# The spectrum's product in the tokens stage, second component made by ScalarE and GpSimd instead of VectorE

## The chip, the cores and the metric

The kernel runs on one core of one Trainium2 chip. The metric is the device time of one execution in microseconds (us). The engines are called PE (TensorE, the matmuls), DVE (VectorE), ACT (ScalarE), POOL (GpSimd) and SP (the queue that issues the DMAs).

## The reference, cut to what matters

The program is a convolution block over 32 images of 96 channels and 56x56 pixels, and then, on each image seen as 3136 tokens of 96 channels, a Fourier mixing layer and an MLP. Only the mixing layer matters here:

```python
h = relu(bn(layernorm(t) @ w1.T))              # 3136 tokens, 192 channels
X = jnp.fft.fft(h, axis=1, norm='ortho')
rd, idg = jnp.diagonal(r), jnp.diagonal(i)
xr = relu(X.real * rd - X.imag * idg + rb)
xi = relu(X.imag * rd + X.real * idg + ib)
y = ifft(xr + 1j * xi).real
o = bn(y @ w2.T)
```

h is real, so the spectrum is computed for half of the frequencies, and the other half follows from its conjugate: each product is needed with a plus and with a minus sign (a sum and a difference).

## The kernel before, in words

Up to 2700 us of the profiled execution the program sets up its constants and does the convolution. The rest is the tokens stage (`tokens_stage`, L1037). It is a software pipeline over the images: the work of one image is spread over five turns (`LAGS`), and in each turn every engine does a part of up to five images. The order on each engine is written out by hand: `PLACES` (L980) gives every step its places in a plan of 2000 slots a turn, and `tensor_turn`, `scalar_turn`, `pool_turn` and `vector_turn` walk through the slots and issue what stands there, modulo 2000. An engine works strictly in that order; semaphores hold it wherever an input is not ready. A turn is marked in this text by its first L1239 matmul.

The spectrum of an image comes in six groups (`XG`, L1111): groups 0, 2, 3 have 8 frequencies of 128 channels, group 5 has 5 of them, groups 1 and 4 ("wide") hold the 64 other channels of two frequencies in one slot, 8 and 7 slots. A slot is 56 numbers per partition, so groups have 448, 448, 448, 448, 392 and 280 numbers. For each group:

- PE (`spectrum_tensor`, L1299; matmuls L1311 for wide groups, L1314 for the others) writes real and imaginary parts to the PSUM tensor `bank_x`, of which there is one. It waits until the group before has been read out of it (`sd_done`, L1306).
- ACT (`scaled_scalar`, L1410) reads the real part and writes two scaled copies with bias to `d_minus` (L1415, L1417).
- DVE (`real_vector`, L1573) adds the scaled imaginary part, with plus to `s_plus` (L1580) and with minus in place in `d_minus` (L1582), for the first and then for the second component: four `scalar_tensor_tensor`, each with one PSUM and one SBUF input.
- ACT (`relu_scalar`, L1420; L1425) takes the ReLU of both halves of `s_plus`.
- DVE (`fold_vector`, L1585; L1593, twice a group) folds `d_minus` and `s_plus` into `zp` or `zq`: both inputs are in SBUF.

Other steps that the text speaks of:

- PE: `w1_tensor` L1359, `stage1_tensor` L1368, `w2_tensor` L1322/L1323, `stage3_tensor` L1329, `stage4_tensor` L1339, layer norm sums L1239, L1244, L1257, L1263, `mlp1_tensor` L1296, `mlp2_tensor` L1350, and `spread_tensor` L1269, which spreads a row of means (`mrow`, `spread_mean_tensor`, needs the MLP's copies `h16_done`) or of reciprocal deviations (`rrow`, `spread_rstd_tensor`, L1283, needs `xc_done`) over the channels.
- DVE: `centre_vector` (`xc`, L1629), `norm_vector` (`yq`, L1638), `bias1_vector` (L1605), `relu1_vector` (L1612), `residual_vector` (`tb`, L1648), `var_vector` (L1597, L1599), `rt` (L1624), copies `wz` L1672 and `cc` L1680.
- ACT: `h16_scalar` L1432, `bn3_scalar` L1507, `squares2_scalar` L1469, `h_scalar` L1501, `a_scalar` L1494, `std1_scalar` L1442.
- POOL has two steps only: `prep_pool` (L1551), after `bn3_scalar`, and `out_pool` (L1559), each a `tensor_tensor` with both inputs in SBUF.

Of the kernel before, what the change touches and what calls it, by code (L numbers as in the profile page):

```python
# [17 lines left out]
ALU = mybir.AluOpType  # L18
ACT = mybir.ActivationFunctionType
# [8 lines left out]
W = 56  # L28
# [11 lines left out]
TP = 2 * W  # L40
# [11 lines left out]
def wait_count(eng, sem, value):  # L52

    if isinstance(value, int) and value <= 0:
        return
    eng.wait_ge(sem, value)
# [44 lines left out]
def build(nc, x4, cw1, g1, b1, cw2, g2, b2, cw3, g3, b3, aw1, bn1g, bn1b, bn1m, bn1v, ar, ai, arb, aib,  # L101
# [13 lines left out]
    with keep:  # L115
# [857 lines left out]
        with st:  # L973
            tokens_stage(nc, st, NB, x, out, z3_d, t_d, a_d, c_d, t1_d, t4_d, g2_d, g3_d, mean_w, s3, w1a, w2p, w2q,
                         w2shift, diag, fq1, fq2, fqb1, fqb2, epsc)
# [22 lines left out]
 'spectrum': (3861, 3995, 4323, 4618, 4907, 5029),  # L998
 'act_scaled': (3910, 4039, 4372, 4679, 4947, 5091),
 'dve_real': (3935, 4127, 4412, 4705, 4969, 5312),  # L1000
 'act_relu': (4002, 4174, 4506, 4752, 5011, 5379),
 'dve_fold': (4027, 4238, 4646, 4926, 5125, 5398),
 'w2': (4475, 4707, 4851, 5070, 5391, 5570, 5667, 5811),
# [33 lines left out]
def tokens_stage(nc, st, NB, x, out, z3_d, t_d, a_d, c_d, t1_d, t4_d, g2_d, g3_d, mean_w, s3, w1a, w2p, w2q, w2shift,  # L1037
                 diag, fq1, fq2, fqb1, fqb2, epsc):

    def sb(name, shape, dt=F32):  # L1040
        return st.enter_context(nc.sbuf_tensor(name, shape, dt))

    def sem(name):
        return st.enter_context(nc.semaphore(name))
# [15 lines left out]
    bt = sb("bt", [TP, KH, H])  # L1060
    sp_t = sb("s_plus", [128, 2, 2, 8, W])
    dm_t = sb("d_minus", [128, 2, 2, 8, W])
    zp = sb("zp", [128, 2, 8, TP])
    zq = sb("zq", [128, 8, TP])
    wz = sb("wz", [TP, 2, 4 * C])
# [15 lines left out]
        for k, n in (("w1", 1), ("s1", 1), ("x", 2), ("c", 1), ("o", 1), ("l0", 1), ("l1", 1))]  # L1081
    LL = (L0, L1)
    xs = X[:, :, :].rearrange("p a (s c) -> p (a s) c", c=128)
# [10 lines left out]
    x_full, ace_done, s0_done, sd_done, s1p_done, d1_done, r_done, z_done = (  # L1094
        sem(k) for k in ("spectrum", "spectrum_scaled", "sum_real", "diff_real", "sum_imag", "diff_imag", "relu_plus",
                         "z_done"))
# [14 lines left out]
    XG = ((0, 0, 8), (1, 0, 8), (0, 8, 8), (0, 16, 8), (1, 8, 7), (0, 24, 5))  # L1111
# [3 lines left out]
    def here(s, name, live):  # L1115
        return [(at[name].index(s + NT * lag), lag) for lag in range(len(live))
                if live[lag] and s + NT * lag in at[name]]
# [181 lines left out]
    def spectrum_tensor(pe, m, g):  # L1299
        wide, k0, n = XG[g]  # L1300
        if wide:
            for k in ((0, 1), (2, 3))[k0 // 8]:
                pe.wait_ge(ld_b[k], m * 16 + 16)
        else:
            pe.wait_ge(ld_b[k0 // 8], m * 16 + 16)
        wait_count(pe, sd_done, m * 6 + g)  # L1306
        for s in range(n):
            if wide:
                for e in range(2):
                    k1 = min(2 * (k0 + s) + e, KH - 1)  # L1310
                    ins = nc.tensor.matmul(xs[64 * e:64 * e + 64, s, 0:TP], bt[:, k1, 128:192], g2c[:, :],  # L1311
                                           start=True, stop=True)
            else:
                ins = nc.tensor.matmul(xs[:, s, 0:TP], bt[:, k0 + s, 0:128], g2c[:, :], start=True, stop=True)  # L1314
        ins.then_inc(x_full, 1)
# [56 lines left out]
    def tensor_turn(pe, tau, par, live):  # L1372
        for s in range(NT):
            for p, lag in here(s, "spread_mean", live):
                spread_mean_tensor(pe, tau - lag, p)
            for p, lag in here(s, "spread_rstd", live):
                spread_rstd_tensor(pe, tau - lag, p)
            for k, lag in here(s, "mlp1", live):
                mlp1_tensor(pe, tau - lag, k)
            for g, lag in here(s, "spectrum", live):  # L1380
                spectrum_tensor(pe, tau - lag, g)
            for c, lag in here(s, "stage4", live):
                stage4_tensor(pe, tau - lag, c)
            for r, lag in here(s, "mean1", live):
                mean1_tensor(pe, tau - lag, (par + lag) % 2, r)
            for r, lag in here(s, "square1", live):
                square1_tensor(pe, tau - lag, r)
            for r, lag in here(s, "mean2", live):
                mean2_tensor(pe, tau - lag, r)
            for r, lag in here(s, "square2", live):  # L1390
                square2_tensor(pe, tau - lag, r)
            for c, lag in here(s, "mlp2", live):
                mlp2_tensor(pe, tau - lag, c)
            for u, lag in here(s, "w2", live):
                w2_tensor(pe, tau - lag, u)
            for u, lag in here(s, "stage3", live):
                stage3_tensor(pe, tau - lag, u)
            for g, lag in here(s, "stage1", live):
                stage1_tensor(pe, tau - lag, g)
            for g, lag in here(s, "w1", live):  # L1400
                w1_tensor(pe, tau - lag, (par + lag) % 2, g)
# [8 lines left out]
    def scaled_scalar(act, m, g):  # L1410
        wide, k0, n = XG[g]
        re = xs[:, 0:n, 0:W]
        act.wait_ge(x_full, m * 6 + g + 1)
        wait_count(act, z_done, (m * 6 + g - 1) * 2)
        nc.scalar.activation(dm_t[:, g % 2, 0, 0:n, :], re, ACT.Identity, bias=diag[:, wide, 2:3],  # L1415
                             scale=diag[:, wide, 0:1]).then_inc(ace_done, 1)
        nc.scalar.activation(dm_t[:, g % 2, 1, 0:n, :], re, ACT.Identity, bias=diag[:, wide, 3:4],  # L1417
                             scale=diag[:, wide, 1:2]).then_inc(ace_done, 1)

    def relu_scalar(act, m, g):  # L1420
        wide, k0, n = XG[g]
        act.wait_ge(s0_done, m * 6 + g + 1)
        act.wait_ge(s1p_done, m * 6 + g + 1)
        v = sp_t[:, g % 2, :, 0:n, :]
        nc.scalar.activation(v, v, ACT.Relu).then_inc(r_done, 1)  # L1425
# [118 lines left out]
    def prep_pool(pool, n, par, c):  # L1544
        pool.wait_ge(bn3_done, n * NCH + c + 1)
        if c == 0:
            wait_count(pool, w1_full, (n - 1) * NG)
            wait_count(pool, st_t, (n - 1) * 16)
        to = y[0:C, par, :, ROWS * c:ROWS * c + ROWS, :].rearrange("p j a b -> p a j b")
        v, xv = (q[:, c % 3, :].rearrange("p (a j b) -> p a j b", a=ROWS, b=2) for q in (zin, xin))  # L1550
        nc.gpsimd.tensor_tensor(to, v, xv, ALU.add).then_inc(y_done, 1)  # L1551

    def out_pool(pool, b, c):
        pool.wait_ge(ob_done, b * NCH + c + 1)
        if c == 0:
            wait_count(pool, st_out, b * 16)
        to = onat[:, :, 8 * c:8 * c + 8].rearrange("p a (j b) -> p j a b", b=2)
        v, o = (q.rearrange("p (j a b) -> p j a b", j=4, b=2) for q in (tb[:, c * CH:c * CH + CH], o16[:, c % 4, :]))
        nc.gpsimd.tensor_tensor(to, v, o, ALU.add).then_inc(out_done, 1)  # L1559

    def pool_turn(pool, tau, par, live):
        for s in range(NT):
            for c, lag in here(s, "pool_y", live):
                prep_pool(pool, tau - lag, (par + lag) % 2, c)
            for c, lag in here(s, "pool_out", live):
                out_pool(pool, tau - lag, c)

    @block.gpsimd
    def _(pool):
        turns(pool, pool_turn)  # L1570


    def real_vector(dve, m, g):  # L1573
        wide, k0, n = XG[g]
        dve.wait_ge(ace_done, (m * 6 + g + 1) * 2)
        wait_count(dve, z_done, (m * 6 + g - 1) * 2)
        im = xs[:, 0:n, W:TP]
        for k, plus, sums, diffs in ((0, 1, s0_done, d1_done), (1, 0, s1p_done, sd_done)):
            v = dm_t[:, g % 2, k, 0:n, :]
            nc.vector.scalar_tensor_tensor(out=sp_t[:, g % 2, k, 0:n, :], in0=im, scalar=diag[:, wide, plus:plus + 1],  # L1580
                                           in1=v, op0=ALU.mult, op1=ALU.add).then_inc(sums, 1)
            nc.vector.scalar_tensor_tensor(out=v, in0=im, scalar=diag[:, wide, 4 + k:5 + k], in1=v, op0=ALU.mult,  # L1582
                                           op1=ALU.add).then_inc(diffs, 1)

    def fold_vector(dve, m, g):  # L1585
        wide, k0, n = XG[g]
# [159 lines left out]
```

## Time and profile before

| | us |
|---|---|
| median of 3 runs (lowest, highest) | 5704.41 (5702.91, 5705.4) |
| the profiled execution's own time | 5686.37 |
| its span, first to last instruction | 5684.6 |

| engine | busy us | share of the span |
|---|---|---|
| PE | 5213.9 | 92% |
| DVE | 3813.3 | 67% |
| ACT | 3411.5 | 60% |
| POOL | 2111.4 | 37% |

Busy shares are means over stages with different limits. The mean TensorE clock granted over the span is 0.934 of full speed; full speed is 2.4 GHz, and the other level is 1.2 GHz.

### The profile page before, as it was taken

The page shows a single profiled execution, that of the slowest core. Times are in us where ns is not written, and L with a number is a line of the kernel's source. Part 1 is how long each engine was busy: PE and PEld are TensorE (multiplying, and loading weights), DVE is VectorE, ACT ScalarE, POOL GpSimd, SP SyncE. Part 2 cuts the span into 40 slices and gives each one's busy share as a digit, 9 for nine tenths or more (in the row PEclk, how much of TensorE's full clock was granted, in tenths as well). Part 3 has the DMA queues.
Part 4 walks back from the last instruction along what each step waited for, and adds up shares of the span by engine and source line. Part 5 has one row for each costly group of instructions (what it writes and reads, how often), then busy time and mean ns, then how long its engine had stood idle before and what let it go on. Part 6 is the DMA issues. An engine that isn't in the chain of part 4 may idle for free.

```text
span 5684.6 us, 146458 instructions
## 1 busy us (share of the span) xinstructions
PE 5213.9 (92%) x59604; PEld 3484.0 (61%) x59604; DVE 3813.3 (67%) x6799; ACT 3411.5 (60%) x5674; POOL 2111.4 (37%) x1092
## 2 busy tenths in 40 slices
PE   4979999999999969999589999999999999999996
PEld 4966666666666634444366676666676766766663
DVE  2036666666666666767257777877777777777775
ACT  1445555555555558888256666666666666666653
POOL 0037777777777736666211111111111111111111
PEclk9989999999999989999689899999988998999986
DMA  3646666666666669999456656656556565565551
GB/s 79 158 115 163 171 168 161 171 170 169 171 163 168 153 254 414 415 411 416 132 148 171 163 152 177 165 158 174 155 159 164 159 165 164 152 177 160 163 133 45
DMA packets 493783, 1041.28 MB, mean 183 GB/s; under 512 B 176464, under 2 KB 345232, under 8 KB 460112
## 3 DMA queue, kind: packets, MB, share of 16 engines
q1 hardware_dynamic: 493120, 1031.92, 62.9%
q8 instruction: 479, 7.85, 0.6%
q14 instruction: 184, 1.51, 0.1%
HBM read 552.39 MB, written 478.94 MB: 181 GB/s over the span
## 4 chain that ended last, share of the span: by engine, by line
PE 40%; ACT 3%; DVE 3%; DMA 2%; issue 2%; SPq 0%; POOL 0%; DVEq 0%; POOLq 0%; ACTq 0%
PE bank_w L1359 6%; PE bank_s L1368 5%; PE bank_l L1269 4%; PE bank_x L1314 4%; PE bank_c L1322 3%; PE bank_o L1339 3%; PE bank_c L1323 3%; PE bank_o L1350 2%; PE bank_c L1329 2%; PE bank_l L1296 2%; ACT h L1432 2%; PE bank_x L1311 1%; PE bank_l L1257 1%; PE bank_l L1263 1%; DMA c_scratch<-cc 1%
## 5 line engine op out<-in xcount | busy, mean ns | idle before, releaser
L720 POOL TENSOR_TENSOR hlo<-h,hhi 128x1682 f16<-128x1682 f32 x288 | 977.2, 3393 | 449.2 <-DVE hhi L751 449.2
L735 DVE BATCH_NORM_STATS2 stats<-z 128x6 f32<-128x392 f32 x1152 | 597.3, 561 | 519.0 <-ACT z L672 509.1
L682 ACT ACTIVATE h<-c1ps,s 128x1512 f32<-128x1512 f32 x288 | 465.1, 1615 | 697.2 <-PE c1ps L598 697.2
L1551 POOL TENSOR_TENSOR y<-zin,x_tok 96x448 f32<-96x448 f32 x224 | 263.4, 1176 | 1341.7 <-ACT zin L1507 1340.1
L619 PE MATMUL dwps<-hhi,taps 64*64 64x392 f16 x13824 | 689.0, 330 | 3.7 <-issue 3.6
L619 PE MATMUL dwps<-hlo,taps 64*64 64x392 f16 x13824 | 681.3, 327 | 1.9 <-issue 1.8
L1559 POOL TENSOR_TENSOR onat<-tb,o 96x448 f32<-96x448 f32 x224 | 240.9, 1075 | 1113.9 <-DVE o L1618 1113.9
L870 ACT ACTIVATE z2m<-z2m,s 128x784 f32<-128x784 f32 x512 | 489.6, 1029 | 107.0 <-DMA z2m<-z_scratch 106.6
L894 POOL TENSOR_TENSOR h_split<-z2m,h_split 128x1568 f16<-128x1568 f32 x128 | 405.0, 3164 | 300.8 <-DVE h_split L933 300.8
L619 PEld LDWEIGHTS dwps<-hlo,taps 64*64 64x64 f16 x13824 | 406.1, 106 | 179.5 <-issue 3.3
L619 PEld LDWEIGHTS dwps<-hhi,taps 64*64 64x64 f16 x13824 | 381.8, 106 | 176.6 <-issue 6.3
L1501 ACT ACTIVATE h<-bank_w,rt 112x192 f32<-112x192 f32 x896 | 325.7, 417 | 252.8 <-PE bank_s L1368 129.8
L1432 ACT ACTIVATE h<-bank_l 128x448 f16<-128x448 f32 x672 | 341.8, 543 | 195.8 <-PE bank_l L1296 193.7
L1359 PE MATMUL bank_w<-w1a,y 97*112 97x193 f32 x1792 | 421.1, 361 | 37.9 <-DMA y<-va 23.1
L598 PE MATMUL c1ps<-xhi,t1h 96*32 96x504 f16 (+1 forms) x4608 | 403.2, 340 | 27.1 <-POOL xlo L665 21.9
L1368 PE MATMUL bank_s<-h,t1c 112*128 112x192 f32 x1792 | 395.7, 345 | 5.1 <-ACT a L1494 5.1
L1359 PEld LDWEIGHTS bank_w<-w1a,y 97*112 97x112 f32 x1792 | 308.4, 194 | 122.9 <-ACT h L1501 72.1
L906 PE MATMUL pps<-z2m,w3T 128*96 128x392 f32 x1024 | 363.5, 498 | 15.2 <-ACT z2m L870 15.2
L665 POOL TENSOR_TENSOR xlo<-xin,xhi 96x448 f16<-96x448 f32 x224 | 233.8, 1045 | 361.2 <-ACT xhi L659 361.2
L598 PE MATMUL c1ps<-xlo,t1h 96*32 96x504 f16 (+1 forms) x4608 | 364.9, 337 | 2.1 <-issue 2.1
L1322 PE MATMUL bank_c<-w2p,zp 128*112 128x96 f32 x1856 | 346.8, 269 | 12.7 <-DVE cc L1680 12.7
L1580 DVE SCALAR_TENSOR_TENSOR s_plus<-bank_x,diag,d_minus 128x448 f32<-128x448 f32 (+2 forms) x384 | 245.5, 639 | 163.7 <-ACT d_minus L1417 163.1
(223 smaller groups left out, 10695.1 us busy)
## 6 DMA issues: line engine op xcount, KB each, us to landing
z_scratch<-z SPq DMA_DIRECT2D x1152, 196.0 KB, 3.3
z2m<-z_scratch SPq DMA_DIRECT2D x64, 1960.0 KB, 15.7
z2m<-z_scratch SPq DMA_DIRECT2D x64, 1568.0 KB, 11.4
a_scratch<-a SPq DMA_DIRECT2D x224, 384.0 KB, 2.8
bt<-a_scratch SPq DMA_DIRECT2D x96, 672.0 KB, 8.9
c_scratch<-cc SPq DMA_DIRECT2D x128, 336.0 KB, 4.3
d<-c_scratch SPq DMA_DIRECT2D x128, 336.0 KB, 4.6
xa<-in_x_dram SPq DMA_DIRECT2D x32, 1176.0 KB, 7.4
```

What stands on the lines that cost most here:

```text
L598: ins = nc.tensor.matmul(c1[32 * q:32 * q + 32, k, 0:cols], t1h[:, 64 * u + 32 * g:64 * u + 32 * g + 32], part[:, m, rows, :], start=(part ...
L619: ins = nc.tensor.matmul(dw[64 * j:64 * j + 64, r, g, 0:QN], taps[half, u, da, dx, :, :].rearrange("p y c -> p (y c)"), part[half, s, a0:a ...
L682: nc.scalar.activation(to, src, ACT.Relu, bias=s1[:, 1, u:u + 1], scale=s1[:, 0, u:u + 1]).then_inc(h_ready, 1)
L720: nc.gpsimd.tensor_tensor(to, h, hi, ALU.subtract).then_inc(lo_ready, 1)
L735: nc.vector.bn_stats(stats[:, i, v, at:at + 6], z2[:, v % 3, g, r, :]).then_inc(s_stat, 1)
L870: nc.scalar.activation(v, v, ACT.Relu, bias=s2[:, 1, t:t + 1], scale=s2[:, 0, t:t + 1]).then_inc(h2_ready, 1)
L894: nc.gpsimd.tensor_tensor(lo, h32, hi, ALU.subtract).then_inc(lo_ready, 1)
L906: nc.tensor.matmul(banks[m], w3T[:, t, :], z2m[:, c // 2, 4 * m + t, cols], start=(t == 0), stop=False)
L1322: nc.tensor.matmul(o, zp[:, k1 // 8 % 2, k1 % 8, :], w2p[:, :], start=True, stop=False)
L1359: ins = nc.tensor.matmul(WB[0:TP, 0, e * (H + 1):(e + 1) * (H + 1)], y[:, par, 2 * g + e, :, :].rearrange("p a b -> p (a b)"), w1a[:, :], ...
L1368: ins = nc.tensor.matmul(SB[:, 0, e * H:e * H + H], t1c[:, 2 * g + e, :], h[:, g % 2, e * H:e * H + H], start=True, stop=True)
L1432: nc.scalar.activation(h16[:, c % 2, q, :], LL[k % 2][:, 0, 0:CH], ACT.Copy).then_inc(h16_done, 1)
```

## The change

For the second component ACT makes a third copy, the imaginary part times the diagonal, in a new SBUF tile `imag_scaled` (`im_t`), and POOL adds and subtracts it (two `tensor_tensor`, all operands in SBUF). DVE keeps only the first component's two instructions. DVE and POOL now wait for all three copies, and PE's wait for a free `bank_x` is for ACT's third copy and DVE's second instruction. `s1p_done` and `sd_done`, for which the ReLU and the fold wait, now come from POOL. POOL's new step has its own places in the plan, between those of its other steps; no other place changes.

```diff
+ 'pool_imag': (3929, 4060, 4400, 4700, 4960, 5110),
+    im_t = sb("imag_scaled", [128, 2, 8, W])
 (spectrum_tensor)
-        wait_count(pe, sd_done, m * 6 + g)
+        wait_count(pe, ace_done, (m * 6 + g) * 3)
+        wait_count(pe, d1_done, m * 6 + g)
 (scaled_scalar)
+        nc.scalar.activation(im_t[:, g % 2, 0:n, :], xs[:, 0:n, W:TP], ACT.Copy,
+                             scale=diag[:, wide, 0:1]).then_inc(ace_done, 1)
+    def imag_pool(pool, m, g):
+        wide, k0, n = XG[g]
+        pool.wait_ge(ace_done, (m * 6 + g) * 3 + 3)
+        wait_count(pool, z_done, (m * 6 + g - 1) * 2)
+        v, im = dm_t[:, g % 2, 1, 0:n, :], im_t[:, g % 2, 0:n, :]
+        nc.gpsimd.tensor_tensor(sp_t[:, g % 2, 1, 0:n, :], v, im, ALU.add).then_inc(s1p_done, 1)
+        nc.gpsimd.tensor_tensor(v, v, im, ALU.subtract).then_inc(sd_done, 1)
 (pool_turn, between pool_y and pool_out)
+            for g, lag in here(s, "pool_imag", live):
+                imag_pool(pool, tau - lag, g)
 (real_vector)
-        dve.wait_ge(ace_done, (m * 6 + g + 1) * 2)
+        dve.wait_ge(ace_done, (m * 6 + g) * 3 + 3)
         wait_count(dve, z_done, (m * 6 + g - 1) * 2)
         im = xs[:, 0:n, W:TP]
-        for k, plus, sums, diffs in ((0, 1, s0_done, d1_done), (1, 0, s1p_done, sd_done)):
-            v = dm_t[:, g % 2, k, 0:n, :]
-            nc.vector.scalar_tensor_tensor(out=sp_t[:, g % 2, k, 0:n, :], in0=im, scalar=diag[:, wide, plus:plus + 1],
-                                           in1=v, op0=ALU.mult, op1=ALU.add).then_inc(sums, 1)
-            nc.vector.scalar_tensor_tensor(out=v, in0=im, scalar=diag[:, wide, 4 + k:5 + k], in1=v, op0=ALU.mult,
-                                           op1=ALU.add).then_inc(diffs, 1)
+        v = dm_t[:, g % 2, 0, 0:n, :]
+        nc.vector.scalar_tensor_tensor(out=sp_t[:, g % 2, 0, 0:n, :], in0=im, scalar=diag[:, wide, 1:2], in1=v,
+                                       op0=ALU.mult, op1=ALU.add).then_inc(s0_done, 1)
+        nc.vector.scalar_tensor_tensor(out=v, in0=im, scalar=diag[:, wide, 4:5], in1=v, op0=ALU.mult,
+                                       op1=ALU.add).then_inc(d1_done, 1)
```

## Rows read from the trace of the kernel before

**Rows 1.** Busy time by stretch: us, then each engine's busy us (count), PE clock, DMA share

```profile
3400.00:4000.00 600.00, 563.83 (x3850) 407.64 (x3849) 470.98 (x934) 398.45 (x773) 112.70 (x99) 0.95 0.60 166
3523.07:3608.41 85.34, 80.56 (x545) 57.60 (x545) 66.91 (x132) 56.13 (x109) 15.46 (x14) 0.93 0.60 164
4214.73:4303.49 88.76, 84.98 (x545) 61.13 (x544) 66.80 (x132) 56.60 (x109) 15.49 (x14) 0.88 0.59 158
2921.13:5427.89 2506.76, 2368.75 (x15775) 1709.53 (x15774) 1936.59 (x3827) 1633.63 (x3160) 456.91 (x405) 0.92 0.60 163
```

**Rows 2.** What PE waited for between 2921.13 and 5427.89: us in total, times, longest

```profile
PE bank_o L1339 <- DVE tb L1648: 20.0, 23, 1.4
PE bank_x L1311 <- DVE d_minus L1582: 19.3, 12, 1.7
...
PE bank_l L1269 <- ACT h L1432: 13.7, 29, 0.5
```

**Rows 3.** Groups of instructions, 3400 to 5200 us: count, busy us, mean ns

```profile
L1582 DVE SCALAR_TENSOR_TENSOR d_minus<-bank_x,diag,d_minus 128x448 f32<-128x448 f32 x166 | 112.1, 675 | 0.0
L1417 ACT ACTIVATE d_minus<-bank_x,diag 128x448 f32<-128x448 f32 x83 | 59.6, 718 | 0.0
L1481 ACT ACTIVATE mrow<-bank_l 128x448 f32<-128x448 f32 x21 | 11.2, 533 | 0.0
```

**Rows 4.** The page's groups on POOL, whole span: count, busy us, mean ns

```profile
L720 POOL TENSOR_TENSOR hlo<-h,hhi 128x1682 f16<-128x1682 f32 x288 | 977.2, 3393 | 449.2 <-DVE hhi L751 449.2
...
L1559 POOL TENSOR_TENSOR onat<-tb,o 96x448 f32<-96x448 f32 x224 | 240.9, 1075 | 1113.9 <-DVE o L1618 1113.9
```

**Rows 5.** Timeline around a fold (start us, us); last, durations of L1582 (ns min/median/max)

```profile
4043.42 1.63 DVE L1593 SCALAR_TENSOR_TENSOR zp<-d_minus,s_plus 128x448 f32<-128x448 f32 x2 [0.51 <-ACT s_plus L1425]
...
4067.82 1.15 DVE L1593 SCALAR_TENSOR_TENSOR zp<-d_minus,s_plus 128x448 f32<-128x448 f32 x2
...
4043.00 1.04 POOL L1559 TENSOR_TENSOR onat<-tb,o 96x448 f32<-96x448 f32 x1 [9.46 <-DVE o L1618]
...
L1582 DVE SCALAR_TENSOR_TENSOR d_minus<-bank_x,diag,d_minus x349: 493/674/678, 2923.2 to 5430.0; 128x448 f32<-128x448 f32 x117, 128x392 f32<-128x392 f32 x29, 128x280 f32<-128x280 f32 x29
```

**Rows 6.** Timeline of ACT in one turn, group 5 and what follows

```profile
3658.07 0.59 ACT L1417 ACTIVATE d_minus<-bank_x,diag 128x280 f32<-128x280 f32 x1
3658.55 0.54 ACT L1432 ACTIVATE h<-bank_l 128x448 f16<-128x448 f32 x1
3659.39 0.98 ACT L1432 ACTIVATE h<-bank_l 128x448 f16<-128x448 f32 x2 [0.30 <-PE bank_l L1296]
```

**Rows 7.** Timeline of DVE in the same stretch

```profile
3658.83 1.03 DVE L1593 SCALAR_TENSOR_TENSOR zq<-d_minus,s_plus 128x392 f32<-128x392 f32 x2
3659.78 0.16 DVE L1624 RECIPROCAL rt<-bank_w 112x2 f32<-112x2 f32 x1
3659.86 0.88 DVE L1605 TENSOR_SCALAR h<-h,fqb 128x448 f16<-128x448 f16 x3
3660.66 0.85 DVE L1612 TENSOR_SCALAR hq<-h 128x1344 fp8e5<-128x1344 f16 x1
3661.47 1.16 DVE L1605 TENSOR_SCALAR h<-h,fqb 128x448 f16<-128x448 f16 x1
3662.58 1.15 DVE L1629 TENSOR_TENSOR xc<-tb,bank_l 96x448 f32<-96x448 f32 x2
```

**Rows 8.** Timeline of POOL in the same stretch

```profile
3661.09 1.41 POOL L1551 TENSOR_TENSOR y<-zin,x_tok 96x448 f32<-96x448 f32 x1 [4.00 <-ACT zin L1507]
```

**Rows 9.** Timeline of PE: the same stretch, then the same place in a longer turn

```profile
3664.00 0.99 PE L1269 MATMUL bank_l<-rrow,row 1*96 1x448 f32 x4
3664.92 0.77 PE L1350 MATMUL bank_o<-hq,fq 128*96 128x448 fp8e5 x3
...
4093.62 1.39 PE L1269 MATMUL bank_l<-rrow,row 1*96 1x448 f32 x4
4094.93 1.35 PE L1350 MATMUL bank_o<-hq,fq 128*96 128x448 fp8e5 x3
```

**Rows 10.** Timeline of ACT and PE after group 2, then after group 4

```profile
4057.24 0.72 ACT L1417 ACTIVATE d_minus<-bank_x,diag 128x448 f32<-128x448 f32 x1
4058.10 1.70 ACT L1469 ACTIVATE sq<-tb 96x1792 f32<-96x1792 f32 x1
...
4060.13 0.94 PE L1263 MATMUL bank_l<-sq,mean_w 96*32 96x448 f32 x8
...
3652.44 0.73 ACT L1501 ACTIVATE h<-bank_w,rt 112x192 f32<-112x192 f32 x2
...
3653.68 0.82 PE L1359 MATMUL bank_w<-w1a,y 97*112 97x193 f32 x4
```

## The prediction

> **What bounds the kernel now.** I read the busy time by stretch first, then PE's waits in the tokens stage, then the timelines of one turn. Only the tokens stage is touched. There PE is busy 564 of 600 us while DVE is at 471, ACT at 398 and POOL at 113 [rows 1]: PE's order sets the pace, and an instruction taken off DVE is worth only what PE waits for DVE. Between 2921.13 and 5427.89 us there are 29 full turns (the reader can count them by the wait of L1269, which occurs 29 times [rows 2]); 2506.76/29 = 86.44 us a turn. PE's idle time is 2506.76 - 2368.75 = 138 us, 4.8 us a turn. That is all that could be won at an unchanged clock. Two waits in it belong to DVE's products: L1311 for the last `d_minus` (12 times, 19.3 us) and L1339 for `tb` (23 times, 20.0 us) [rows 2].
>
> Turns come in two lengths with the same instructions: 85.34 us at a mean granted clock of 0.93 and 88.76 us at 0.88, and the longer one has less PE idle time (88.76 - 84.98 = 3.8 us against 4.8) [rows 1]. So the 3.4 us between them are slow matmuls: in the longer turn the stretch that begins with the spread of `rrow` runs L1269 and L1350 in 1.39 and 1.35 us instead of 0.99 and 0.77 [rows 9], which is the level of 1.2 GHz against 2.4 GHz in part of them. The mean of 86.44 means about (86.44 - 85.34)/3.42 = a third of the turns at the longer length.
>
> **The change part by part.** Times inside a group are counted from the end of ACT's second copy.
>
> *DVE, two instructions fewer.* At 675 ns each [rows 3], issued some 0.6 us apart, six groups a turn: 8 us less busy a turn, worth nothing by itself as DVE has 130 us free in 600.
>
> *ACT, one copy more.* The second copy of 448 takes 718 ns with scale and bias; a plain copy of 448 from PSUM takes 533 ns [rows 3]. The new one, a copy with a scale, is between them; I take the upper end, 0.6 us from issue to issue as its neighbours. At group 5, 0.47 us.
>
> *Release of `bank_x` and of DVE.* Before, four DVE instructions: about 2.5 us. After, the third copy 0.6 and two DVE instructions 1.3: 1.9 us. Both come 0.57 us earlier at best. Where L1311 waits, 12 of 29 turns, PE gains 0.57: 0.24 us a turn. `tb` follows the product of group 1 on DVE's queue; but a SBUF-only instruction (L1599) stands between and meets POOL's new pair, so I take 0.3 us in 23 of 29 turns: 0.24 us. Bounds for the two together: 0 and (12 x 0.57 + 20.0)/29 = 0.9 us a turn.
>
> *ReLU and fold.* The ReLU needs POOL's first instruction. On POOL, 448 numbers take 1.03 to 1.08 us and 1682 take 3.39: 1.9 ns a number, so about 0.72 us for 280, 0.93 for 392 [rows 4]. ReLU input is ready at 0.6 + 1.05 = 1.65 us, against about 1.9 before (DVE's third); the fold's input at 2.7 against 2.5, and the fold waits for the ReLU anyway. Nothing on the path. POOL has room: 113 of 600 us, and the new pairs add about 12 us a turn.
>
> *ACT's copy in front of other ACT work.* After group 2 the squares start 0.14 us after the second copy ends and end at 4059.80; PE takes them up at 4060.13 [rows 10]. The third copy moves their end to about 4060.3: 0.2 us. After group 4, L1501 ends at 3653.17, moves to about 3653.77 and is needed by L1359 at 3653.68 [rows 10]: 0.1 us. After group 5 the copy sits ahead of the MLP's copies, 0.47 us, of which an idle 0.30 us of ACT [rows 6] swallows most: 0.2 us into the spread of `mrow`, which already waits 0.47 us in each turn [rows 2]. This one is hidden under the next term.
>
> *POOL's pair against DVE's SBUF instructions.* This decides. First the row: a fold pair takes 1.15 us alone and 1.63 us when it starts beside a POOL instruction that has 0.62 us to run [rows 5]; DVE's products, which have one input in PSUM, show no such tail: 349 of them with a median of 674 and a maximum of 678 ns [rows 5]. The last L1605 takes 1.16 us (about 0.3 alone, three take 0.88) beside L1551, and L1551 itself takes 1.41 us because L1612 was running when it asked [rows 7, 8]. So the two hold each other off for whole instructions, and who asked first goes first.
>
> The Trainium skill, page "SBUF — State Buffer", section "Who interferes with whom", says that the second to issue is blocked fully, for a DVE instruction in a two-port mode or with two SBUF inputs against a GpSimd one that reads SBUF. By it the fold pair of the row should have lost 0.62 us; it lost 0.48, because some of its start-up is covered.
>
> Now group 5. Its third copy ends at 3659.1, POOL asks at 3659.15, and exactly there DVE runs the fold of group 4, three L1605, L1612, another L1605 and then `xc` [rows 7]. In turns: fold one to 3659.39; POOL 0.72 to 3660.1; fold two 0.47 to 3660.6; POOL 0.72 to 3661.3; one L1605 0.3 to 3661.6; L1551 (it asks near 3661.3) 1.13 to 3662.75; two L1605 to 3663.3; L1612 0.8; L1605 0.3; the two `xc` 1.07: end at 3665.5. Before it was 3662.58 + 1.15 = 3663.73, and PE's spread of `rrow`, which needs `xc`, starts at 3664.00 without a wait [rows 7, 9]. So the cover is 0.27 us and DVE is 1.75 late: PE waits about 1.5 us; with the 0.14 us start-up found in the row, twice, it is 1.2 us, and I take 1.3. This place is the same in every full turn. Lower bound 0.2 us (only ACT's delay) if the two share; 0.4 us if L1551 comes last; upper 2.2 us if POOL holds once more.
>
> The skill's full block, taken by itself, would make this term 1.5 and the sum 6 us larger.
>
> *Sum at an unchanged clock:* 1.3 + 0.2 + 0.1 - 0.24 - 0.24 = +1.1 us a turn, 32 us in 29 turns.
>
> *Clock.* The new wait lies right ahead of the stretch that is at 1.2 GHz in the longer turns and not in the shorter ones. A PE that stands still there makes the slow stretch likelier; I take it that all turns go to 88.8 us: (88.8 - 86.44) x 29 = 68 us, in which the 32 are contained. The profiled execution's 5686.4 + 68 = 5754 us. The median of the runs is 18 us above that execution, about five more long turns by 3.4 us; if so these are no longer there to be added. I forecast 5755.
>
> **Rivals.**
> - *The port is met but PE's clock does not follow:* +1.1 us a turn, 32 us: 5704 + 32 = 5736. For it: turns of either length exist with the same waits. Chance 0.25, the full case 0.42 (both are my mechanism).
> - *It evens out.* POOL's pair is fitted between without costing `xc` more than 0.3 us (L1551 last, or shorter POOL instructions), against the two gains of 0.24: within 10 us of 5704. Chance 0.15.
> - *Faster.* One mechanism: `bank_x` and DVE come free 0.57 us earlier, the waits L1311 and L1339 shrink, and the slow stretch loses its trigger so that all turns are 85.3: 1.1 x 29 = 33 us, 5671. It decides if `xc` is less than 0.27 us late. Against it: the fold of group 4 stands exactly where POOL's pair lands. Chance 0.13.
> - *Much slower:* 2.2 us at group 5 and turns of over 90 us: 29 x 3.8 = 110 us, 5797 to 5815. Chance 0.05.
>
> **The numbers.** The range from 5695 to 5810 leaves out the faster rival and the end of the last, under 2 in 10. A measurement of this kernel can tell about 0.2% (11 us). Slower by more than that: 0.42 + 0.25 + 0.05 = 0.72; within: 0.15; faster: 0.13. The likeliest case's own range is 5725 to 5785.
>
> **What would show it.** In the changed profile, in each full turn: the `rrow` spread L1269 after group 5 waits for `xc` 1 to 1.5 us (before: no wait); the folds of group 4 take 1.7 us or more a pair; POOL's instructions of group 5 show lengths over 0.72 us; L1311's longest wait falls from 1.7 to 1.1 us; a turn is 88.8 us and the clock about 0.88. Wrong: no wait of PE for `xc`, or turns of 85.3 us. If the `xc` wait is there and turns stay near 87.5, the clock step alone was wrong.

## The result, and the profile after

| | before | after |
|---|---|---|
| median, lowest and highest of 5 runs, us | 5705.40 (5702.91 to 5722.83) | 5741.18 (5729.77 to 5746.02) |
| ratio after/before, 95% interval | | 1.0049 [1.0028, 1.0070] |
| span of the profiled execution, us | 5684.6 | 5730.0 |
| mean granted clock | 0.934 | 0.929 |

The change makes the kernel slower, by 36 us between the medians, 45 us between the profiled executions. One execution among all those of this text, one of e3's twelve, took 6615.6 us at a mean granted clock of 0.75 and is left out of the ratios. Lines of the changed kernel stand a few numbers later: L1311 is now L1314, L1339 is L1342, L1269 is L1271, L1593 is L1607, L1605 is L1619, L1629 (`xc`) is L1643, and the turn's mark L1239 is L1241.

First the busy time by stretch (us, then PE, PEld, DVE, ACT, POOL, clock, DMA share and GB/s): the 29 full turns, then a short and a long turn.

```profile
2911.28:5473.66 2562.38, 2406.57 (x15774) 1727.83 (x15773) 1799.13 (x3479) 1712.14 (x3334) 823.52 (x753) 0.91 0.58 160
3352.53:3437.63 85.10, 80.36 (x546) 56.96 (x545) 61.63 (x120) 58.98 (x115) 28.44 (x26) 0.95 0.58 159
3615.37:3707.82 92.45, 87.12 (x546) 62.17 (x545) 61.71 (x120) 59.25 (x115) 28.50 (x26) 0.87 0.56 154
```

A turn is 2562.38/29 = 88.36 us, against 86.44 [rows 1]: 1.92 us more, 56 us in all. (Ahead of the first full turn the profiled execution is 10 us faster than before: that stretch begins at 2911 instead of 2921.) PE's idle time grew from 138.0 to 2562.38 - 2406.57 = 155.8 us, by 17.8; PE's busy time, for the same matmuls, by 37.8 us. So in this pair of executions two thirds of the difference are slower matmuls. But the profiled execution of the kernel before is one of its quicker ones, with a mean clock of 0.934 where the 76 on record beside the experiments have 0.930; "All executions on one line" below gives the clock a smaller part. DVE is relieved, 1936.59 to 1799.13 us, and that bought nothing.

What PE waited for in the 29 turns (us in total, times, longest):

```profile
PE bank_o L1342 <- DMA d<-c_scratch: 34.2, 19, 4.4
PE bank_w L1362 <- DMA y<-va: 25.5, 19, 2.6
PE bank_l L1271 <- issue: 18.5, 29, 1.0
PE bank_o L1342 <- DVE tb L1662: 14.6, 20, 0.8
...
PE bank_x L1314 <- DVE d_minus L1596: 9.4, 10, 1.0
PE bank_l L1271 <- ACT h L1437: 9.3, 29, 0.4
```

The two waits for a DMA in the kernel before, which [rows 2] leave out:

```profile
PE bank_o L1339 <- DMA d<-c_scratch: 23.3, 17, 2.4
...
PE bank_w L1359 <- DMA y<-va: 19.2, 16, 1.9
```

Against [rows 2], `bank_x` (19.3 to 9.4), `tb` (20.0 to 14.6) and the spread of `mrow` (13.7 to 9.3) gave 20 us. A new wait took 18.5 us, 29 times, and the DMAs of `d` and of the row of `y` 10.9 and 6.3 us more. The profile names no engine for the new one ("issue"). Its place names it: in each of the 29 turns the spread of `rrow` starts 0.10 us after the end of `xc`. The same stretch as in [rows 6 to 9], in the short turn: ACT, DVE, POOL, PE, in that order.

```profile
3403.05 0.60 ACT L1420 ACTIVATE d_minus<-bank_x,diag 128x280 f32<-128x280 f32 x1
3403.52 0.51 ACT L1422 ACTIVATE imag_scaled<-bank_x,diag 128x280 f32<-128x280 f32 x1
...
3404.05 1.03 DVE L1607 SCALAR_TENSOR_TENSOR zq<-d_minus,s_plus 128x392 f32<-128x392 f32 x2
3405.01 0.16 DVE L1638 RECIPROCAL rt<-bank_w 112x2 f32<-112x2 f32 x1
3405.09 2.66 DVE L1619 TENSOR_SCALAR h<-h,fqb 128x448 f16<-128x448 f16 x3
3407.67 0.85 DVE L1626 TENSOR_SCALAR hq<-h 128x1344 fp8e5<-128x1344 f16 x1
3408.44 0.32 DVE L1619 TENSOR_SCALAR h<-h,fqb 128x448 f16<-128x448 f16 x1
3408.68 1.14 DVE L1643 TENSOR_TENSOR xc<-tb,bank_l 96x448 f32<-96x448 f32 x2
...
3404.11 1.61 POOL L1563 TENSOR_TENSOR s_plus<-d_minus,imag_scaled 128x280 f32<-128x280 f32 x1 [2.05 <-ACT imag_scaled L1422]
3405.68 0.81 POOL L1564 TENSOR_TENSOR d_minus<-d_minus,imag_scaled 128x280 f32<-128x280 f32 x1
3406.45 1.17 POOL L1556 TENSOR_TENSOR y<-zin,x_tok 96x448 f32<-96x448 f32 x1
...
3409.92 0.99 PE L1271 MATMUL bank_l<-rrow,row 1*96 1x448 f32 x4 [0.63 <-issue]
```

POOL asks at 3404.11, while the fold pair runs, and needs 1.61 us for 280 numbers (0.77 in e1 below, where no fold runs beside it; 1.61 is the median of the 29 turns). Then three L1619 take 2.66 us instead of 0.88 [rows 7], beside three POOL instructions that follow one another without a gap. One by one these three are:

```profile
3405.09 0.77 DVE L1619 TENSOR_SCALAR h<-h,fqb 128x448 f16<-128x448 f16 x1
...
3405.78 0.84 DVE L1619 TENSOR_SCALAR h<-h,fqb 128x448 f16<-128x448 f16 x1
...
3406.54 1.21 DVE L1619 TENSOR_SCALAR h<-h,fqb 128x448 f16<-128x448 f16 x1
```

Each of them ends 0.13 or 0.14 us after one of POOL's three (at 3405.72, 3406.49 and 3407.61): one POOL instruction holds up one of DVE. `xc` ends 6.17 us after the second copy of group 5 (3403.65 to 3409.82); before it was 5.07 (3658.66 to 3663.73). So it is 1.1 us later, PE stands still 0.63 us in front of the spread of `rrow`, and the spread starts 6.27 us after that copy instead of 5.34.

### The profile page after: what moved, and what is told of

It is laid out like the page before. It is cut to its first block, busy times and chain, and to the rows that moved or that the text cites. A ratio compares the mean times of both kernels' runs of the same rounds, so it can differ in the third digit from the quotient of the medians.

```text
span 5730.0 us, 146904 instructions
## 1 busy us (share of the span) xinstructions
PE 5253.3 (92%) x59604; PEld 3503.5 (61%) x59604; DVE 3663.4 (64%) x6415; ACT 3497.6 (61%) x5866; POOL 2517.0 (44%) x1476
## 4 chain that ended last, share of the span: by engine, by line
PE 40%; ACT 4%; DMA 3%; issue 3%; DVE 2%; SPq 1%; POOL 0%; DVEq 0%; POOLq 0%; ACTq 0%
PE bank_w L1362 6%; PE bank_s L1371 5%; PE bank_l L1271 4%; PE bank_x L1317 4%; PE bank_o L1342 3%; PE bank_c L1325 3%; PE bank_c L1326 3%; PE bank_o L1353 2%; PE bank_c L1332 2%; PE bank_l L1298 2%; ACT h L1437 2%; PE bank_l L1259 1%; PE bank_l L1265 1%; DMA y<-va 1%; PE bank_x L1314 1%
## 5 line engine op out<-in xcount | busy, mean ns | idle before, releaser
L720 POOL TENSOR_TENSOR hlo<-h,hhi 128x1682 f16<-128x1682 f32 x288 | 977.1, 3393 | 448.7 <-DVE hhi L751 448.7
L1563 POOL TENSOR_TENSOR s_plus<-d_minus,imag_scaled 128x448 f32<-128x448 f32 (+1 forms) x192 | 227.2, 1183 | 740.1 <-ACT imag_scaled L1422 740.1
L1556 POOL TENSOR_TENSOR y<-zin,x_tok 96x448 f32<-96x448 f32 x224 | 255.5, 1141 | 516.0 <-ACT zin L1512 515.9
L1362 PE MATMUL bank_w<-w1a,y 97*112 97x193 f32 x1792 | 432.8, 369 | 47.1 <-DMA y<-va 29.8
L1619 DVE TENSOR_SCALAR h<-h,fqb 128x448 f16<-128x448 f16 x672 | 287.3, 443 | 133.1 <-ACT h L1437 116.7
```

What stands on the lines that cost most here:

```text
L720: nc.gpsimd.tensor_tensor(to, h, hi, ALU.subtract).then_inc(lo_ready, 1)
L1362: ins = nc.tensor.matmul(WB[0:TP, 0, e * (H + 1):(e + 1) * (H + 1)], y[:, par, 2 * g + e, :, :].rearrange("p a b -> p (a b)"), w1a[:, :], ...
```

## The experiments

Each was timed in 5 rounds, 6 to 12 executions, against the kernel before on the same chip. The changed kernel itself was not timed again beside them, so it is compared with them by the ratios. "Idle" and "busy" are PE's, in the 29 full turns of one profiled execution. Executions of one kernel differ by up to 50 us (the kernel before beside e1 to e4: 5672 to 5723), so the medians decide, and the idle and busy columns are only a hint.

| run | median | before beside it | ratio [95%] | idle | busy | wait at `rrow` | wait for `d` |
|---|---|---|---|---|---|---|---|
| before | 5705.4 | | | 138.0 | 2368.8 | none | 23.3 |
| changed | 5741.2 | 5705.4 | 1.0049 [1.0028, 1.0070] | 155.8 | 2406.6 | 18.5 | 34.2 |
| e1 pair of group 5 later | 5733.9 | 5703.6 | 1.0048 [1.0028, 1.0067] | 147.1 | 2417.7 | 13.4 | 33.8 |
| e2 `xc` late by 1.2 | 5768.8 | 5703.6 | 1.0099 [1.0070, 1.0129] | 165.9 | 2419.9 | 24.2 | 21.4 |
| e3 third copy alone | 5709.8 | 5703.6 | 1.0006 [0.9992, 1.0021] | 144.4 | 2381.0 | none | 35.3 |
| e4 relief alone | 5687.5 | 5703.6 | 0.9964 [0.9946, 0.9983] | 157.1 | 2362.1 | none | 63.7 |
| e5 group 5 back | 5698.7 | 5709.1 | 0.9987 [0.9970, 1.0004] | 156.7 | 2354.3 | none | 55.1 |
| e6 e5 and loads later | 5661.6 | 5709.1 | 0.9933 [0.9906, 0.9960] | 139.3 | 2338.6 | none | 23.0 |
| e7 loads later alone | 5714.8 | 5709.1 | 1.0008 [0.9994, 1.0023] | 129.5 | 2402.2 | none | 1.6 |
| e8 idle pair | 5744.1 | 5709.1 | 1.0053 [1.0032, 1.0074] | 159.9 | 2407.3 | 16.1 | 27.0 |
| e9 `xc` late by 0.3 | 5705.7 | 5702.2 | 1.0007 [0.9989, 1.0025] | 134.5 | 2411.7 | 0.2 | 19.8 |
| e10 changed, loads later | 5705.7 | 5702.2 | 1.0000 [0.9982, 1.0017] | 150.8 | 2364.4 | 18.5 | 19.9 |

**All executions on one line.** For every execution its time and its mean granted clock are known, so the two parts of a difference can be told apart better than from one profile. The 76 executions of the kernel before (clocks 0.922 to 0.937) lie on a straight line of time against 1/clock with a scatter of 3 us; by its slope 0.001 of clock is worth 4 us. The height of a run's executions above that line is what it costs at an equal clock, with an error of some 2 us; this is an estimate, since the waits and the clock may not be independent.

| run | us above the line | mean clock |
|---|---|---|
| e2 | 33 | 0.924 |
| changed | 27 | 0.928 |
| e8 | 24 | 0.927 |
| e1 | 22 | 0.929 |
| e10 | 14 | 0.934 |
| e3 | 12 | 0.933 |
| e5 | 8 | 0.933 |
| e9 | 1 | 0.929 |
| e4 | -1 | 0.935 |
| e7 | -4 | 0.926 |
| e6 | -6 | 0.938 |

So most of the changed kernel's 36 us is there at an equal clock, and 19 of the 27 go with the pair of group 5 (e5, below). The lower clock, 0.928 against 0.930, is worth 7 us, with an error of 4.

**e1, the pair of group 5 one step later.**

```diff
- 'pool_imag': (3929, 4060, 4400, 4700, 4960, 5110),
+ 'pool_imag': (3929, 4060, 4400, 4700, 4960, 5250),
```

> The changed kernel with one place moved: GpSimd's pair of group 5 goes from slot 5110 to 5250, behind the step that adds the residual of the last chunk. Port theory (the pair holds VectorE's SBUF work off in front of xc; PE waits 0.64 us a turn for it and its clock falls): that wait is gone, turns fall from 88.4 towards 86.5 us, the time returns to 5705 or somewhat below (the other pairs' relief is kept): 5680 to 5715. Rival, ScalarE's third copy costs the time: the wait may go but the time stays within 10 us of 5741. Rival, the clock is luck: PE idle falls by 0.64 us a turn, 19 us, and no more: 5722.

Measured 5733.9: 1.0048 as the changed kernel, so the time missed the forecast. But the wait was not removed, only cut to 13.4 us. Its timelines of DVE, POOL and PE say why:

```profile
3410.82 1.90 DVE L1619 TENSOR_SCALAR h<-h,fqb 128x448 f16<-128x448 f16 x1
3412.64 1.14 DVE L1643 TENSOR_TENSOR xc<-tb,bank_l 96x448 f32<-96x448 f32 x2
...
3410.43 1.42 POOL L1556 TENSOR_TENSOR y<-zin,x_tok 96x448 f32<-96x448 f32 x1 [4.24 <-ACT zin L1512]
...
3411.81 0.77 POOL L1563 TENSOR_TENSOR s_plus<-d_minus,imag_scaled 128x280 f32<-128x280 f32 x1
3412.55 0.81 POOL L1564 TENSOR_TENSOR d_minus<-d_minus,imag_scaled 128x280 f32<-128x280 f32 x1
...
3413.88 0.99 PE L1271 MATMUL bank_l<-rrow,row 1*96 1x448 f32 x4 [0.46 <-issue]
```

In a plan that only orders an engine's instructions, "later" meant right behind L1556, and the one L1619 in front of `xc` now waits for two POOL instructions, 1.90 us. This run left the theory untested, and called for taking the pair away (e5) or adding it alone (e8).

**e2, a late `xc` without any of the change:** an idle `reciprocal` of 170 columns ahead of it.

```diff
+        if c == 2:
+            nc.vector.reciprocal(idle[:, :], full[:, :]).then_inc(s_idle, 1)
         nc.vector.tensor_tensor(xc[:, c % 2, :], tb[:, c * CH:c * CH + CH], ...
```

> The kernel before with one idle reciprocal of 170 columns (about 1.1 us) on VectorE ahead of xc of chunk 2, just after group 5, and nothing else. It makes xc late by what the changed kernel shows (1.1 us) with GpSimd and ScalarE as before. Port theory with the clock following the wait: PE waits 0.8 to 0.9 us a turn at that place, turns of 88 us, time 5740 to 5765 (more than the 26 us that the wait itself makes). Clock-is-luck rival: 5705 + 0.85 x 29 = 5730 at most, mean clock as before. If the late xc is no cause: 5705.

```profile
PE bank_l L1271 <- issue: 24.2, 29, 1.1
```

0.83 us a turn, as forecast, and 5768.8, just above the forecast: 65 us more than before, of which the wait is 24. The same "issue" label appears at the same place, so the new wait of the changed kernel is the one for `xc`. At an equal clock e2 is 33 us slower; the rest is its low clock (0.924).

**e9, a third of that delay:** 40 columns instead of 170, a reciprocal of 0.40 us instead of 1.22.

> As the late centre, but the idle reciprocal has 40 columns instead of 170: about 0.3 us instead of 1.2. The prediction put the cover of xc at 0.27 us. If the cover is right, PE waits 0.1 us a turn or less for the rrow spread and the time is within 10 us of the kernel before (5705), where the 170 columns cost 65 us. If every delay of xc costs (no cover): a quarter of that, 16 us or more, 5720.

5705.7 and no wait (0.2 us once in 29 turns). There is a cover of about 0.27 us, as [rows 7, 9] had it; a delay of about that size costs nothing that can be measured. Its profiled execution, 5725 us, has as long a busy time as the changed kernel's, without the wait: the busy time of one execution proves nothing on the clock.

**e8, the contention alone.** In the kernel before, POOL does two idle `tensor_tensor` of 280 numbers at the place of group 5's pair; VectorE and ScalarE do all that they did.

```diff
+                if g == 5:
+                    pool.wait_ge(ace_done, ((tau - lag) * 6 + g) * 2 + 2)
+                    nc.gpsimd.tensor_tensor(idle[:, :], full[:, :], full[:, :], ALU.add).then_inc(s_idle, 1)
+                    pool.wait_ge(s_idle, (tau - lag) * 2 + 2)
+                    nc.gpsimd.tensor_tensor(idle[:, :], full[:, :], full[:, :], ALU.subtract).then_inc(s_idle, 1)
+                    ...
```

> The kernel before with an idle pair of GpSimd instructions (280 numbers, two SBUF inputs from a constant tile, unused output) at the place of the changed kernel's pair of group 5, and nothing else: VectorE still makes all products, ScalarE two copies. It is the contention alone. Port theory: xc comes 1 us late, PE waits 0.5 to 0.8 us a turn for the rrow spread and the time is 5725 to 5760 as with the late xc. If the port costs nothing: 5705.

```profile
3408.89 2.59 DVE L1616 TENSOR_SCALAR h<-h,fqb 128x448 f16<-128x448 f16 x3
...
3407.76 1.64 POOL L1571 TENSOR_TENSOR idle<-full 128x280 f32<-128x280 f32 x1 [1.65 <-ACT d_minus L1420]
...
3413.65 0.99 PE L1272 MATMUL bank_l<-rrow,row 1*96 1x448 f32 x4 [0.56 <-issue]
```

Two instructions of which nobody uses a result reproduce the picture (1.64 us on POOL, 2.59 on DVE, 0.56 of waiting) and the loss: 1.0053 against 1.0049. e8 and e9 are the fair pair for the wait: their profiled executions have the same clock in the 29 turns (0.91) and nearly the same busy time, and 159.9 against 134.5 us idle. So the contention alone makes a loss as large as the change's.

**e5, group 5 given back to VectorE,** with two ScalarE copies and nothing on POOL; groups 0 to 4 keep the change.

```diff
- 'pool_imag': (3929, 4060, 4400, 4700, 4960, 5110),
+ 'pool_imag': (3929, 4060, 4400, 4700, 4960),
 (scaled_scalar)
+        if g < 5:
+            nc.scalar.activation(im_t[:, g % 2, 0:n, :], xs[:, 0:n, W:TP], ACT.Copy, ...
 (real_vector)
+        if g == 5:
+            ...
+            nc.vector.scalar_tensor_tensor(out=sp_t[:, g % 2, 1, 0:n, :], ... .then_inc(s1p_done, 1)
+            nc.vector.scalar_tensor_tensor(out=v, ... .then_inc(sd_done, 1)
```

> The changed kernel, but group 5 is done as before: two ScalarE copies, four VectorE instructions, nothing on GpSimd. Groups 0 to 4 keep the change. Port theory: xc is back in time, the wait of L1271 for the rrow spread (0.64 us a turn, still 0.46 with the pair one step later, since one L1619 then stood behind two GpSimd instructions, 1.90 us) is gone, and the time is 5690 to 5710, the changed kernel's loss removed. Rival, the other five groups cost as much (DMA waits, ScalarE's copies, slow turns): 5725 to 5745.

5698.7, the wait at `rrow` gone, and by the ratios 0.6%, some 35 us, under the changed kernel. Taking the pair away removes the loss, adding it makes it. In the sum the other five groups cost nothing, but their relief is not seen either (0.9987, interval over 1): the wait for `d` is 55.1 us.

**e3, the third copy alone.** As before, with one more ScalarE activation a group, from a constant in SBUF into an unused tile.

> The kernel before with a third ScalarE copy a group, of the same size, from a constant in SBUF into an unused tile; VectorE waits for the first two only, and makes all four products. It isolates ScalarE's time. If ScalarE's copy is the cause: 5730 or more. By my sum (0.2 us at the squares, 0.1 at L1359, 0.2 at the spread of mrow): 0.5 us a turn, 15 us, 5720. Port theory needs it small: 5705 to 5725.

```profile
L1420 ACT ACTIVATE imag_scaled<-t4c,diag 128x448 f32<-128x448 f32 x82 | 54.4, 664 | 0.0
```

1.0006: ScalarE takes 0.66 us for it and the time does not change at the level of 0.2%. At an equal clock e3 is 12 us slower, near the 15 us that the sum gave to this copy, and its clock of 0.933 gives that back; why the clock is higher stays open.

**e4, the relief alone.** VectorE's two instructions of the second component are left out, with nothing in their place: the second component is then computed without its imaginary part, so the output is another. (Not shown: the waits for their semaphores, which go too, and a constant for the unused half.)

```diff
-        for k, plus, sums, diffs in ((0, 1, s0_done, d1_done), (1, 0, s1p_done, sd_done)):
+        for k, plus, sums, diffs in ((0, 1, s0_done, d1_done),):
```

> The kernel before with VectorE's two instructions of the second component left out (the spectrum's second component is then computed without its imaginary part, so the output is another), no third copy and nothing on GpSimd. It gives what the relief of VectorE is worth at best. Release of bank_x comes 1.2 us earlier. If VectorE's load mattered: the waits L1311 (19.3 us) and L1339 for tb (20 us) vanish, 5665 or below. If the DMA of d, which lands 10.5 us after the turn's mark whatever PE does, takes their place: gain under 20 us, 5685 to 5705.

```profile
PE bank_o L1340 <- DMA d<-c_scratch: 63.7, 22, 5.5
...
PE bank_o L1340 <- DVE tb L1647: 8.4, 15, 0.8
...
PE bank_x L1312 <- DVE d_minus L1582: 7.4, 15, 0.5
```

Even a relief that costs nothing gains only 16 us of 5704 (10 to 31 by the interval). `bank_x` and `tb` fall by 23.5 us against [rows 2], and the wait for `d` rises by 40: PE comes to `stage4_tensor` earlier and finds the DMA not there. At an equal clock e4 is as fast as before; the 16 us are its higher clock (0.935).

**e6, e7, e10: what stands in front of `d`.** On SP's queue, around the turn's mark at 3792.80 of the changed kernel:

```profile
3791.45 0.42 SPq L1173 DMA_DIRECT2D c_scratch<-cc  x1
3791.98 0.49 SPq L1168 DMA_DIRECT2D bt<-a_scratch  x1
3792.52 2.74 SPq L1149 DMA_DIRECT2D zin<-z_scratch  x1
3795.32 1.37 SPq L1150 DMA_DIRECT2D x_tok<-in_x_dram  x1
3798.39 0.30 SPq L1180 DMA_DIRECT2D d<-c_scratch  x1
```

The load of `d` is issued 0.08 us after the store of `cc` has landed (median of the 29 turns; the same before, in the changed kernel and in e5, e6, e7 and e10), and loads of other images are issued between the two. The edit moves the first chunk's loads (L1149, L1150) behind the load of `d`:

```diff
-PLACES = {'load_in': (0, 143, 286, 429, 571, 714, 863),
+PLACES = {'load_in': (48, 143, 286, 429, 571, 714, 863),
```

e6 is e5 with it, e7 the kernel before with it, e10 the changed kernel with it.

> As group 5 back on VectorE, and the loads of the next image's first chunk (zin, x_tok) are issued behind the load of d instead of ahead of it (slot 0 to 48). If the wait of L1339 for d, which grew as others shrank (23 us before, 34 changed, 64 with the relief alone), comes from the traffic in front of it, it falls by a half, and the time is 10 to 20 us under the run without it: 5675 to 5700. If d's own store and load set it: no difference within 5 us.

> The kernel before with only that place of the loads moved (slot 0 to 48). If traffic delays d: the wait of 23 us for d shrinks to about 10, 5690 to 5700. Otherwise 5705.

> The changed kernel with only the place of the first chunk's loads moved (slot 0 to 48). With group 5 back on VectorE the same move took the time from 5699 to 5662; in the kernel before it did nothing, since other waits took the place of d's. Here the wait for d is 34 us and the wait for the rrow spread (18.5 us) stays: if the two are independent, the gain is as there, 5700 to 5715; if the rrow wait with its slow turns sets the pace, under 10 us, 5730 to 5741.

The wait for `d` in e5, e6 and e7:

```profile
PE bank_o L1342 <- DMA d<-c_scratch: 55.1, 23, 5.1
```

```profile
PE bank_o L1342 <- DMA d<-c_scratch: 23.0, 14, 2.9
```

```profile
PE bank_w L1359 <- DMA y<-va: 31.5, 22, 2.7
PE bank_o L1339 <- DVE tb L1648: 29.5, 28, 1.9
...
PE bank_o L1339 <- DMA d<-c_scratch: 1.6, 3, 0.8
```

e6 takes 5661.6 us: 0.9933 [0.9906, 0.9960], faster than both kernels, and 37 us under e5, where 10 to 20 were forecast; 14 of them are there at an equal clock. e10 brings the changed kernel back to the time of the one before, 36 us, so the gain adds to the loss at `xc` rather than hiding behind it. e7, with VectorE as loaded as before, gains nothing, which missed its forecast: the wait for `d` falls from 23.3 to 1.6 us, but those for `tb` and for the row of `y` rise from 20.0 and 19.2 to 29.5 and 31.5. That is not the whole of it, since its idle time is still 8.5 us shorter, and at an equal clock it is 4 us faster; a clock of 0.926 takes that away. So by the medians the relief and the earlier load are worth something only together, and what part of that is the clock's stays open.

What the move shortens is the transfer of `d` itself. The first load of `d` in a turn takes, from issue to landing, 5.3 us in the kernel before, the changed one and e5, and 3.7, 3.8 and 3.65 us in e7, e10 and e6 (medians of the 29 turns). The store of `cc` takes 5.6 to 6.0 us in all six, so it is not what was delayed, and neither is the issue of the load. Whether the two moved loads slow it by their traffic or by standing ahead of it in the queue was not separated.

## Why the prediction was right, and where its steps were off

- *Sign, place and cause.* Right. The measured 5741 lies in 5725 to 5785; the pair of group 5 meets VectorE's SBUF instructions, and `xc` comes late in each of the 29 turns. e8 and e5 show it from both sides, e9 and e2 show the cover and what lies beyond it.
- *The size at group 5* was twice too large: 1.3 us a turn forecast, 0.64 measured, `xc` late by 1.1 instead of 1.75 us. The order was wrong: I let POOL in between the two folds; both folds ran through in 1.03 us, unstretched, and POOL waited (1.61 us). But the order is not what made the term too large, since three POOL instructions were to hold VectorE up and three did. The step that failed is the price of one such meeting. I charged 0.72, 0.72 and 1.13 us, nearly POOL's whole instructions; the three L1619, which take 0.32 to 0.34 us each before, took 0.77, 0.84 and 1.21, so they lost 0.45, 0.5 and 0.9. The fourth, which had stood behind L1551 before (1.16 us), took 0.32, as I had it.
- *The rule of the Trainium skill,* page "SBUF — State Buffer", section "Who interferes with whom": a fully blocked second instruction. The trace agrees: each held L1619 ends just behind a POOL instruction. As a sum (1.5 us) it was further off than my 1.3. It names the parties, it did not give the time.
- *VectorE's relief:* 8 us less busy a turn forecast, 4.7 measured. e4, which takes the same two instructions away and puts nothing on POOL, has 5.8: some 1.1 us a turn went back into stretched instructions. Nothing in the sum hung on it.
- *Release of `bank_x`.* 0.57 us forecast; the longest wait went from 1.7 to 1.0, the total fell by 9.9 us (forecast 0.24 x 29 = 7). *`tb`:* 5.4 us, forecast 7. Both right, but I did not ask what comes next and put it at nothing: the DMA of `d`, +10.9 us, and the row of `y`, +6.3, took all of it in the profiled execution. One execution does not settle these two (e3, without any relief, waits 35.3 us for `d`); the 63.7 and 55.1 us of e4 and e5 do show the exchange. By e4's interval, a relief of VectorE alone gains at most 31 us.
- *ScalarE's copy:* 0.63 us for 448 numbers, between the bounds of 0.533 and 0.718 [rows 3]. The 0.3 us a turn that I gave it do not show in PE's waits of the changed kernel; e3 shows 12 us at an equal clock and nothing in its median.
- *POOL's instructions:* 0.77, 1.02 and 1.14 us for 280, 392 and 448 numbers; forecast 0.72, 0.93, 1.05. Between them that is 2.2 ns a number; the 1.9 came from L720, which writes f16 [rows 4].
- *Sum at an unchanged clock:* 32 us forecast, 17.8 us measured as idle time, 27 by all executions at an equal clock. This is near, but in part by luck: a wait for `xc` of half the forecast (18.5 us for 38) and two DMA waits that were not in the sum (17 us) make up for each other.
- *Clock.* This step failed. All turns were to go to 88.8 us, 68 us in all. Between the medians it is 36 us, of which the lower clock has about 7, so the rival without a clock step (5736) was nearer than the forecast of 5755; 5741 lies within the range of both. The reading under it was too simple as well: of the 29 turns before, 10 take 85.3 us and 6 take 88.8, and the other 13 lie anywhere from 83.1 to 88.3. In the changed profile they run from 84.2 to 92.5, with a mean of 88.36 and a clock of 0.91, not 0.88. The four runs with a late `xc` (changed, e1, e2, e8) all have a lower clock than 0.930, but clear of their errors only e2 and e8. Against "the wait makes the clock slow" speaks that e10 has the same wait, 18.5 us, and a clock of 0.934, and that e7 has none and 0.926. At an equal clock a wait at this place costs between itself (18.5 us: the changed kernel is 19 over e5, e10 20 over e6) and one and a half times itself (e2 24.2 us: 33; e8 16.1 us: 24); what makes the clock fall in one turn and not in the next stays open.

## What to carry to other kernels

An instruction moved to GpSimd is paid where it meets VectorE's SBUF-only work, not where it stands in the plan: list what VectorE does in the next 3 us and who waits for that. Taking load off an engine that is not the bound gains what PE waits for it, less what comes next in line; here a DMA did, and moving the loads of one chunk behind it turned a relief worth nothing (e5) into 0.7% (e6). One profiled execution can mislead on the clock: set the times of all executions against their granted clocks before giving a loss to it. A test that moves a step in an ordered plan has to be read in the timeline first: in e1 the step moved, the collision did not go away.

## What was not expected of the hardware

- Two queued VectorE instructions with two SBUF inputs went through back to back while a GpSimd instruction waited 0.84 us (1.61 against 0.77); then three GpSimd instructions ran without a gap while three short f16 `tensor_scalar` lost 1.78 us, one held up by each.
- A wait of 0.83 us a turn, 24 us in all, cost 65 us (e2), one of 0.56 us cost 35 us (e8), 33 and 24 us of them at an equal clock, and a delay of 0.3 us, the size of the cover, cost nothing (e9).
- The 76 executions of the kernel before lie on a line of time against 1/clock with a scatter of 3 us, while their clocks range from 0.922 to 0.937 and their times from 5672 to 5733 us.
